# A graph and mixture-of-experts kernel: the recurrent graph stage written out without loops, its transposes and its rounding of V moved

## What is computed

```python
for i in range(weight.shape[0]):          # 5 layers
    m = h @ weight[i]
    msgs = m[src] * edge_attr[:, None]
    agg = jax.ops.segment_sum(msgs, dst, num_segments=n_nodes)
    h = gru_cell(agg, h, w_ih, w_hh, b_ih, b_hh)
```

## Time and profile before

| | us |
|---|---|
| median of 3 runs | 4189.82 (4189.17 to 4216.44) |
| the profiled execution | 4204.7 |
| its span (first to last instruction) | 4203.1 |
| mean granted clock of PE | 0.905 of full speed |

### The profile page before, as it was taken

How to read it: one execution, slowest core, us unless ns; L and a number is a source line. 1 busy time by engine, 2 the same in 40 slices (tenths; PEclk the granted TensorE clock), 3 DMA queues, 4 the chain that set the end, 5 groups by cost and what they waited for, 6 DMA issues and landing times. The chain is left out here.

```text
span 4203.1 us, 58482 instructions
## 1 busy us (share of the span) xinstructions
PE 3130.9 (74%) x17934; PEld 2752.0 (65%) x17935; DVE 2357.0 (56%) x5512; ACT 1257.4 (30%) x2219; POOL 1447.5 (34%) x940
## 2 busy tenths in 40 slices
PE   2555451200999953599958999998999999999598
PEld 2444440100788852499848988987998898899465
DVE  7999991410688773366565545454454555545423
ACT  0000000110444421233324444444444444444132
POOL 1577777667766776776440000000000000000000
PEclk9999995655999985799979999999999999999699
DMA  9755544574666644455335333332333333332100
GB/s 399 252 139 132 129 104 100 127 210 97 191 166 182 173 100 113 117 127 132 80 125 178 128 113 118 121 131 96 132 121 113 118 128 110 128 120 88 40 27 21
DMA packets 378488, 549.07 MB, mean 131 GB/s; under 512 B 127283, under 2 KB 289114, under 8 KB 374234
## 3 DMA queue, kind: packets, MB, share of 16 engines
q1 hardware_dynamic: 242468, 464.88, 32.2%
q0 software_dynamic: 128400, 56.30, 10.2%
q10 hardware_dynamic: 7462, 25.89, 1.7%
HBM read 398.99 MB, written 147.99 MB: 130 GB/s over the span
## 5 line engine op out<-in xcount | busy, mean ns | idle before, releaser
L467 POOL DMA_INDIRECT plane_a<-pair,slot x392 | 653.2, 1666 | 376.7 <-issue 136.9
L467 POOL DMA_INDIRECT plane_w<-pair,slot x392 | 654.0, 1668 | 226.0 <-issue 117.4
L583 PE MATMUL bank<-ring_hi,h_hi 128*128 128x448 f32 x1750 | 661.5, 378 | 79.2 <-DVE ring_lo L1495 79.2
L1495 DVE TENSOR_TENSOR ring_lo<-ring_lo,ring_hi 128x448 fp32r<-128x448 f32 x875 | 525.4, 622 | 241.0 <-ACT ring_hi L1005 240.1
L583 PE MATMUL bank<-ring_lo,h_hi 128*128 128x448 f32 x1750 | 648.7, 371 | 0.0
L583 PE MATMUL bank<-ring_hi,h_lo 128*128 128x448 f32 x1750 | 648.0, 370 | 0.0
L1005 ACT ACTIVATE ring_hi<-ring_lo 128x448 fp32r<-128x448 f32 x875 | 496.7, 577 | 395.7 <-PE bank L583 385.8
L531 POOL DMA_DIRECT2D v_lo<-gru_v x5 | 3.6, 724 | 1386.9 <-PE bank L583 1373.5
L583 PE MATMUL bank<-gring_hi,hs_hi 128*128 128x512 f32 (+2 forms) x700 | 260.0, 371 | 292.6 <-DVE gring_lo L1266 292.6
L583 PEld LDWEIGHTS bank<-ring_hi,h_hi 128*128 128x128 f32 x1750 | 334.0, 191 | 110.9 <-issue 42.8
L556 PE MATMUL bank<-parts,eq 128*128 (+1 forms) x3136 | 132.9, 170 | 317.6 <-DVE hit_hi L1213 316.9
(11 more groups left out here) (302 smaller groups left out, 5966.9 us busy)
## 6 DMA issues: line engine op xcount, KB each, us to landing
ring_lo<-plane_w SPq DMA_DIRECT2D x175, 1120.0 KB, 5.3
gring_lo<-plane_a SPq DMA_DIRECT2D x50, 1280.0 KB
plane_a<-nat SPq DMA_DIRECT2D x25, 1600.0 KB, 45.5
plane_w<-nat SPq DMA_DIRECT2D x100, 400.0 KB
w_hl<-w_split POOLq DMA_DIRECT2D x16, 2048.0 KB
keyrow<-key_rows ACTq DMA_DIRECT2D x49, 512.0 KB
part_in<-in_L_ffn_W SPq DMA_DIRECT2D x16, 1024.0 KB
w_split<-part_hi SPq DMA_DIRECT2D x16, 1024.0 KB, 4.4
```

What stands on the lines that cost most here:

```text
L467: g_.indirect_dma_start(out=plane, out_offset=bass.IndirectOffsetOnAxis(slot[:, t:t + 1], 0), in_=pair[:, k, t:t + 1], in_offset=None, com ...
L583: last = mm(ps, lhs[x], rhs[y], start=start and n == 0, stop=stop and n == 2)
L1495: V.tensor_tensor(ring_lo[:, t, :], ring_lo[:, t, :].bitcast(FP32), ring_hi[:, t % HS, :].bitcast(FP32), ALU.subtract).then_inc(lo_rdy, 1)
```

## The change

The loops over layers and chunks are gone on PE, ACT and DVE: all 34 chunks after the first are written out. SP's and POOL's loops stay. A chunk's sum banks now go by q, not by c, so that they alternate across a layer's edge as well. Turned tiles no longer have banks of their own: tiles 0 to 6 go, as before one after each of the slots 4 to 10, into the sum banks of the coming chunk; tiles 7 to 20 go two after each of the slots 18 to 24 into the four gate banks, and so do tiles 21 to 24 in chunk 0; none is turned in slots 11 to 17. The last layer's tiles go through four banks. The first five ring tiles of the next chunk are made within slots 20 to 24. V is rounded in slot 20 (`TV`) of the next layer's chunk 0.

```diff
+TL, TV = 21, 20
+TE = 7
+TURNS = {**{t: [t - 4] for t in range(4, 4 + TE)}, **{t: [2 * t - 29, 2 * t - 28] for t in range(18, NT)}}
...
+        def turned_tile(i, t):
+            if i == LAYERS:
+                return (sum_ps[1] + sum_ps[0])[t % 4][:, 0:D]
+            if t < TE:
+                return sum_ps[(GC * i) % 2][t % 2][:, 0:D]
+            return gate_ps[(t - (TL if t >= TL else TE)) % 4][:, 0:D]
...
             def turn_back(i, t):
...
-                pe.wait_ge(back_lo, NT * i + t + 1)
+                if t in (TE, TL) and i < LAYERS:
+                    pe.wait_ge(g_act, 2 * (GC * i - (t == TE)) + 1)
+                    pe.wait_ge(g_dve, 2 * (GC * i - (t == TE)) + 1)
+                reused = t - (2 if t < TE and i < LAYERS else 4)
+                if reused >= (TE if TE <= t < TL and i < LAYERS else 0):
+                    pe.wait_ge(back_lo, NT * i + reused + 1)
...
-            def aggregate_w(i, c, par, back=False, turn=False):
+            def aggregate_w(i, c, back=False, turn=False):
                 q = GC * i + c
+                par = q % 2
                 for t in range(NT):
-                    if t == 0 and back:
-                        pe.wait_ge(gT_a, q + 1)
-                        pe.wait_ge(gT_d, q + 1)
-                    if t == 0 and not back:
+                    if t == 0:
                         pe.wait_ge(gT_a, q)
                         pe.wait_ge(gT_d, q)
+                    if t == TA and back:
+                        pe.wait_ge(back_lo, NT * i + TL)
...
-            with pe.Fori(0, LAYERS - 1) as i:
-                chunks_w(i)
-                aggregate_w(i + 1, 0, 0, back=True)
-            chunks_w(LAYERS - 1, more=False)
+            for q in range(1, GC * LAYERS):
+                i, c = divmod(q, GC)
+                aggregate_w(i, c, back=c == 0, turn=c == GC - 1 and i < LAYERS - 1)
...
-            def chunk_w(i, c, par, first=False, turn=False, more=True):
+            def chunk_w(i, c, first=False, turn=False, more=True):
...
                     if t + HS < NT:
                         high(q, t + HS)
+                    elif more:
+                        high(q + 1, t + HS - NT)
...
-                    if turn and t > NT - TL:
-                        back(i + 1, t - 1 - (NT - TL))
-                if first:
-                    round_v(i)
-                if more:
-                    for t in range(HS):
-                        high(q + 1, t)
+                    if turn:
+                        for x in TURNS.get(t - 1, ()):
+                            back(i + 1, x)
+                    if turn and t == NT - 1:
+                        for x in TURNS[t]:
+                            back(i + 1, x)
+                    if first and t == TV:
+                        round_v(i)
```

More of the change, by code:

```diff
@@ L777, in aggregate_w @@
                         gate_products(q - 1, 1)
-                    if turn and t >= NT - TL:
-                        turn_back(i + 1, t - (NT - TL))
-            def chunks_w(i, more=True):
-                with pe.Fori(0, GC // 2 - 1) as m:
-                    for b in range(2):
-                        aggregate_w(i, 2 * m + b + 1, (b + 1) % 2)
-                aggregate_w(i, GC - 2, 1)
-                aggregate_w(i, GC - 1, 0, turn=more)
+                    if turn:
+                        for x in TURNS.get(t, ()):
+                            turn_back(i + 1, x)
             for t in range(NT):
-                pe.wait_ge(back_lo, t + 3)
+                pe.wait_ge(back_lo, t + 1)
                 pe.wait_ge(lo_rdy, t + 1)
@@ L1008, in back @@
                 act.wait_ge(back_ps, NT * (i - 1) + t + 1)
[L1009 removed]
+                A(h_hi[:, t, :], turned_tile(i, t), ACT.Copy).then_inc(back_hi, 1)
             def take_sum(q, par):
@@ L1062, in round_v @@
                 A(v_hi[:, :, :], v_lo[:, :, :].bitcast(FP32), ACT.Copy).then_inc(v_h, 1)
-            def chunks_w(i, more=True):
-                with act.Fori(0, GC // 2 - 1) as m:
-                    for b in range(2):
-                        chunk_w(i, 2 * m + b + 1, (b + 1) % 2)
-                chunk_w(i, GC - 2, 1)
-                chunk_w(i, GC - 1, 0, turn=more, more=more)
             def take_nat(t):
@@ L1093, in _ @@
                 high(1, t)
-            with act.Fori(0, LAYERS - 1) as i:
-                chunks_w(i)
-                chunk_w(i + 1, 0, 0, first=True)
-            chunks_w(LAYERS - 1, more=False)
+            for q in range(1, GC * LAYERS):
+                i, c = divmod(q, GC)
+                chunk_w(i, c, first=c == 0, turn=c == GC - 1 and i < LAYERS - 1, more=q < GC * LAYERS - 1)
             take_sum(GC * LAYERS - 1, 0)
@@ L1522, in new_h, with chunk_w @@
                 V.tensor_tensor(at, gr[:, :, :], gn[:, :, :], ALU.add).then_inc(g_new, 1)
-            def chunk_w(i, c, par, first=False, turn=False, more=True):
+            def chunk_w(i, c, first=False, turn=False, more=True):
                 q = GC * i + c
-                take_sum(q - 1, 1 - par if not first else 0)
-                if first:
-                    back(i, TL - 1)
+                take_sum(q - 1, (q - 1) % 2)
                 for t in range(NT):
@@ L1533, in chunk_w @@
                         low(q, t + HS)
+                    elif more:
+                        low(q + 1, t + HS - NT)
                     for j, at in ((0, TA), (1, TB)):
@@ L1540, in chunk_w @@
                         split_h(q, c)
-                    if turn and t > NT - TL:
-                        back(i + 1, t - 1 - (NT - TL))
-                if first:
-                    rest_of_v(i)
-                if more:
-                    for t in range(HS):
-                        low(q + 1, t)
+                    if turn:
+                        for x in TURNS.get(t - 1, ()):
+                            back(i + 1, x)
+                    if turn and t == NT - 1:
+                        for x in TURNS[t]:
+                            back(i + 1, x)
+                    if first and t == TV:
+                        rest_of_v(i)
             def rest_of_v(i):
@@ L1551, in rest_of_v @@
                 V.tensor_tensor(v_lo[:, :, :], v_lo[:, :, :].bitcast(FP32), v_hi[:, :, :].bitcast(FP32), ALU.subtract).then_inc(v_set, 1)
-            def chunks_w(i, more=True):
-                with ch.loop(0, GC // 2 - 1, 8) as m:
-                    for b in range(2):
-                        chunk_w(i, 2 * m + b + 1, (b + 1) % 2)
-                chunk_w(i, GC - 2, 1)
-                chunk_w(i, GC - 1, 0, turn=more, more=more)
             def combine(t):
@@ L1601, in _ @@
             v.wait_ge(tr_out, 2 * NT)
-            with ch.loop(0, LAYERS - 1, 4 * GC) as i:
-                chunks_w(i)
-                chunk_w(i + 1, 0, 0, first=True)
-            chunks_w(LAYERS - 1, more=False)
+            for q in range(1, GC * LAYERS):
+                i, c = divmod(q, GC)
+                chunk_w(i, c, first=c == 0, turn=c == GC - 1 and i < LAYERS - 1, more=q < GC * LAYERS - 1)
             take_sum(GC * LAYERS - 1, 0)
```

22 lines of the change are left out of this document (9 added, 13 removed).

## The result

The kernel after takes 4,136.5 us (median of 4 executions, 4,126.9 to 4,150.6). In the same session the kernel before took 4,199.7 (4,189.2 to 4,216.4). The ratio is 0.985, with a 95% interval of 0.982 to 0.987: 63 us less by the medians. The profiled execution is the slowest of the four, 4,150.6 us with a span of 4,149.0.

A forecast was written before the change was run, and what follows sets the result against it. PE bounds the recurrent stage, so only its idle and lower-clock time can be won: 50 us at four layer edges plus 5 in the last tiles, 4,189.8 - 55 = 4,135 us, range 4,108 to 4,158.

The forecast's parts named there:

- The floor: One layer edge without waits, 438 matmuls plus 25 turned tiles: 94.4 to 96.2 us, mean 95.3.
- Slots 11 to 17: Chunk 6, nothing turned there any more: the waits of 1.53 and 3.17 us go.
- Slots 18 to 24: Chunk 6, two tiles turned per slot: DVE's debt stalls PE 1.7 us, five later slots 0.3 each; 3.3 us lost per edge.
- Chunk 0's start: Other banks and ring tiles made earlier leave nothing to wait for: the 2.98 us wait goes, 0 counted.
- V in slot 20: Chunk 0: V's rounding goes ahead of turned tiles 23 and 24; PE waits 1.4 to 1.5 us, replacing 1.60.
- The outer edge: Start of chunk 1: without jump, "issue" or table load, the 3.31 us wait before the gates goes; 0 left.
- The edges' sum: Four layer edges: each loses 7.2 us and takes 102.5; together 410 instead of 460, a gain of 50 us.
- The last tiles: Last layer's 25 tiles: four banks cover DVE's idle time, 0.42 us each instead of 0.62; gain 5 us, bounds 0 and 7.
- Loop edges elsewhere: Inner loop edges and register instructions outside the layer edges: 0 gained, as they lie inside unbroken matmul stretches.
- the quick pace holds: Rival, stage outside the edges: straight code without long waits keeps PE at 0.2030 us a matmul; another 21 us, 4,114; chance 0.15.
- VectorE's debt: Rival, slots 18 to 24 lose 8 us at each edge, so 19 us of the gain are lost: 4,154; chance 0.20.
- code waited for: Rival, fresh straight code costs 3.31 us at each of 33 chunk starts, 109 us in all: 4,244; chance 0.05.

The follow-up runs named there:

- Experiment 2: Kernel after, with ACT and DVE copying the previous slot's turned tiles ahead of that slot's high and low parts; four edges 393.9 us, against 405.5.
- Experiment 7: Kernel after, with tiles 7 to 20 turned one in each of slots 11 to 24, still in the gate banks; four edges 418.1 us, against 405.5.
- experiment 3: Kernel after, with tanh, `new_h` and the split of h's second tile pair one slot earlier in every chunk; four edges 398.3 us, against 405.5.
- Experiment 1: Kernel before, with only its chunk and layer loops written out as straight code on PE, ACT and DVE; ratio 0.9965, four edges 447.8 us against 460.4.
- experiments 4 and 5: Kernel after, with V rounded in slot 22 and in slot 24 instead of slot 20; four edges 403.9 and 407.3 us, against 405.5.
- experiment 8: Kernel after, with two banks instead of four for the last layer's turned tiles; closing tiles 15.6 us against 9.0, edges 405.1.
- experiment 9: Kernel after, with turned-tile copies first, h's second pair one slot earlier and V in slot 22; 4,116.2 us, ratio 0.978 to the kernel before.
- experiment 6: Kernel after, with tiles 7 and 8 turned in slot 13 and the other pairs in slots 19 to 24; four edges 404.8 us, against 405.5.

## Why the prediction came out right, step by step

The time and the mechanism came out as forecast, 4,136.5 us against 4,135; some terms did not. That the two times lie 1.5 us apart is luck: the kernel before was 10 us dearer in the session of the result than the 4,189.8 that I started from, and the gain was 63 us and not 55. As a ratio, 55 us less is 0.987, at the upper end of the measured interval: the gain was forecast a little too small.

- *The floor* of 95.3 us an edge: 0.7 too dear. It was the mean of the quick and the slow pace, 94.4 and 96.2. At the quick pace it is 94.3, as worked out, but most stretches of these edges were quick, so the mean was 94.6.
- *Slots 4 to 10*, 1.4: nearly right (1.6). Experiment 2 shows why: the copy stands behind the ring tile on its engines.
- *Slots 11 to 17*: right. The 1.53 and 3.17 are gone and nothing came in their place. Experiment 7, with tiles turned there again, waits 2.78 and 0.74.
- *Slots 18 to 24*, 3.3: too dear. Measured is 2.3. The stall of 1.7 at slot 20 is 1.4, and "another 0.3 each in five slots, 1.6" is 0.9: some 0.4 in every second slot. This is the step that was off most, 1.0 us an edge. Its picture of the stall was also only part of it: I walked VectorE's debt (0.8, experiment 3) and not the copy's place in the queue (0.6, experiment 2).
- *Chunk 0's start* at 0: right. Experiment 1 keeps the old banks and the old place of the ring tiles, and still waits 2.87 there, for the copy of chunk 6's sums behind the ring tiles. Which of the two, other banks or earlier ring tiles, would have been enough is not shown.
- *Slot 19*, 1.0: nearly right (1.3).
- *V in slot 20*, 1.4 to 1.5 at slot 23: nearly right (1.6). As what a late V would hold up, experiments 4 and 5 show `gT_lo`.
- *The outer edge* at 0, and straight code free: right. Experiment 1 gives 12.6 us for it at the edges. But the prediction named the wrong engine: not ACT's 2.38 and its table load held the first gates, but DVE, which stood 4.43 us at the same jump. The Trainium skill (Runtime: NRT & Kernel Launch, section "Instruction fetch mechanics") says that crossing from one block of code to the next in sequence costs little that shows, while a taken branch to a target outside the fetched window must wait for its page; the pieces of 1,188 unbroken matmuls and the vanished 4.43 and 3.31 agree.
- *The edges' sum*: 50 forecast, 54.9 and 52.2 in the two pairs of profiles (54.6 and 53.0 with the pace taken out). An edge takes 101.4, not 102.5: 0.7 of this is the floor, and 0.4 that it loses 6.8 and not 7.2.
- *The last tiles*, 5: the cause is right (experiment 8). The size was 6.6, near the bound of 7, since PE's clock came up halfway; the 5 without it are as forecast.
- *Loop edges elsewhere* at 0: nearly right. The stage's other parts are 11.0 and 3.9 us shorter in the two pairs. 10.2 and 3.0 of this is the pace, and 0.8 and 0.9 are left. The share of slow matmuls in the uninterrupted stretches was 60% and 33% in the two profiles of the kernel before, 21% and 23% in those of the kernel after. The rival "the quick pace holds" is thus half there, but not as I put it: it does not follow from the code's being straight. Experiment 1 had 76% slow, experiment 9 had 57%, experiment 6 none. Its price was also too high. The prediction divides 1,192.9 us by 5,772 matmuls; outside the edges are 5,796 (7,748 less the 200 of the turned tiles and 4 x 438), 0.2058 each, and that is a mixture of the paces and not near the slow one. All quick would then be 16 us less and not 21.

Whether fewer breaks make the slow pace rarer stays open. The three profiles with the old edges averaged 56% slow, the ten with the new ones 23%, but single profiles range from 0 to 57% with edits that hardly differ, and that is too few to settle it. Without the pace the two pairs give 54.6 + 6.6 + 0.8 = 62 and 53.0 + 6.3 + 0.9 = 60 us for the change, against 63 by the medians and my 55. The pace can move a single execution by up to 7,000 x 0.0039 = 27 us in this stage, and the start of the stage moved by 24 us.

In the prediction the stage's 2,234.8 is called the first gates of chunk 1; it is its first matmul, and the windows are cut there in both kernels.

The rival of VectorE's debt fell with 2.3 in place of 8 us, that of code waited for with experiment 1.

## What to carry to other kernels

Split a stretch that repeats into its floor and its waits, and walk each engine's queue at the place of each wait: the waits of one edge were forecast to 0.3 us where rows gave the durations, and to 1.0 where I added a margin per slot. Count a wait from start to start: what the brackets leave out was 2.8 of 6.8 us here. Where a wait is named by nothing, or by an engine long done, look which of the semaphores it waits for came last in the other engines' timelines. Where waits have causes of their own, their cures nearly add up, and ordering the short copy that another engine waits for ahead of the work nobody waits for yet was the cheapest of them (2.9 us an edge, no new buffers). Before reading a gain of 1% from two profiles, profile each kernel twice: here the code ahead of the stage moved the first pair by 17.6 us and the pace by some 10, against a change of 63.

## What was not expected of the hardware

- PE at the full granted clock has two paces for these matmuls of 448 columns, 0.2027 and 0.2066 us from start to start (1.9% apart). An uninterrupted stretch keeps its pace, up to 1,344 matmuls; a new one may have the other, and the same stretch differs from execution to execution. No cause was found.
- Between chunk 1 and chunk 34 the granted clock was at the lower level, in the 13 profiles, behind 27 of PE's 34 waits of 2.78 to 3.34 us (0.56 over 3 us above), and behind none of the 22 of 1.51 to 2.03 us.
- At the jump back of the outer loop DVE stood 4.43 us and ACT 2.38, where the inner loop's jump left PE a gap of 0.2 and DVE none.
- The profile named "issue" as what ended a wait of 0.39 and of 1.65 us, though DVE's `gT_lo` had ended 0.1 us before in both: a wait on several semaphores can be put down to none of them.
